# A Mamba recurrence regrouped: 4 states x 32 channels per partition instead of 2 states x 64

## The chip, the cores and the metric

One core of a Trainium2 chip runs the whole layer. The metric is the device time of one launch in microseconds, the median over runs. TensorE is written PE below, VectorE DVE, ScalarE ACT, GpSimd POOL, and SP is the engine that issues most DMAs.

## The reference

A layer for 2,048 tokens of width 512: a layernorm, then `x + mamba(xn) + moe(xn)`, with a mixture of 64 experts (top 6) and a shared expert. The part in question is the mamba recurrence (1,024 channels, 16 states each):

```python
dt = jax.nn.softplus(dt + dt_proj_b)
def step(state, inp):
    dt_t, x_t, B_t, C_t = inp
    dA = jnp.exp(dt_t[..., None] * A)
    dBx = dt_t[..., None] * B_t[:, None, :] * x_t[..., None]
    state = state * dA + dBx
    y = jnp.einsum('bds,bs->bd', state, C_t)
    return (state, y)
...
y = ys.transpose(1, 0, 2) + xt * D
y = y * jax.nn.silu(gate)
```

## The kernel before

Three stages, one behind the other. `stage1` makes the layernorm, the input projection with its convolution and gate, the router and its token lists. `stage2` runs the recurrence and, woven into it, the routed experts. `stage3` makes the shared expert, the output projection and the sum of everything. The change is in `stage2`.

`stage2` has 32 steps: 4 chunks of 512 tokens by 8 tiles of 128 channels. Each step also works off one pair of experts. On PE the loop is `for cc in 2`, in it two copies of a loop over j (4 passes), in it two steps (u = 0, 1) written out; so one pass of the inner loop is two steps, and the code of the two copies lies one behind the other.

A step holds 8 groups (g), each a tile of 128 partitions by 2 x 512. A partition stands for one channel and one residue of the state: 2 parities of the state by 64 channels, and the group says which half of the channels (b) and which pair of states (m). Per group:

- `dBx` (L1025 to 1036) on PE makes the product dt * x * B for the group: 16 fp32 matmuls of 64x64 tiles, 128 columns each, from the transposed dt*x and diagonals of B into one of two buffers `p_dBx`. It waits for the scan of g-2. Each fp32 matmul is two MATMUL records and two LDWEIGHTS records in the profile.
- ACT makes `dA` = exp(A * dt) (L937) from `dt_halves`, and saves the last column of the state (`state_carry`, L934).
- DVE scans (L842), two instructions a group, into one of four `state` buffers.
- POOL multiplies the state by C (L784) into one of four `h_times_C` buffers; behind group 0 it issues the gather of tokens (L753), behind group 2 the scatter of expert outputs (L765, L769).
- `sum_states` (L1040 to 1047) on PE adds the states with a 0/1 matrix of 128x64 into `p_y`: for each pair of states (m) 4 matmuls of 512 columns, 64 output partitions each.

PE's order in a step i is written out by hand: product 0, sum m=2 of the step before, dt_proj (L985), product 1, the experts' gate (L1005), product 2, sum m=3 of the step before, transpose_h (L1012), product 3, half of `up`, product 4, the other half, product 5, sum m=0, dtx_T (L998), product 6, sum m=1 (it needs POOL's groups 0 to 3), product 7, `down` (L1022), tokens_T (L991).

dt for the next step: dt_proj, softplus on ACT in four operations at g = 3, `next_dt` (L804) on DVE behind scan 2, then `skip` (L818, y += D*x), `next_dtx` (L811) and behind scan 3 `gate` (L824, y * silu(gate)). At g = 6 ACT copies dt into `dt_halves`, each half of the partitions for itself (L892), and issues two DMAs (L897) that bring each half to the other 64 partitions. At g = 7 it takes the transposed dt*x (L902) and makes diagonals of B for the next chunk (L964).

SP issues, per step and in this order, each behind a wait: w_dt and ts of step i+2; w_gate of the next pair; two rows of C (L1385); x for the next dt*x; x and silu(gate) for skip and gate, and the store of the finished y; w_up; w_down.

## Time and profile before

| what | us |
|---|---|
| median of 3 runs | 1509.86 |
| the runs | 1514.99, 1500.84, 1509.86 |
| the profiled execution | 1520.02 |
| its span, first to last instruction | 1518.2 |
| stage 1 | 0 to about 290 |
| stage 2 | about 290 to 1178 |
| stage 3 | about 1187 to the end |
| PE, DVE, ACT, POOL busy over the span | 1393.1, 1101.0, 916.0, 923.9 |

A record of the profile is one instruction; busy time counts overlapping records once, and a group's mean is that of single records, so that side by side tiles have a sum of means far over the busy time. "idle before" is the time in which the engine had nothing running ahead of that group, with what ended it. A step is found in the timeline by PE's products (L1035): eight blocks of 32 matmuls.

### The profile page before, as it was taken

The page shows a single profiled execution, that of the slowest core. Times are in us where ns is not written, and L with a number is a line of the kernel's source. Part 1 is how long each engine was busy: PE and PEld are TensorE (multiplying, and loading weights), DVE is VectorE, ACT ScalarE, POOL GpSimd, SP SyncE. Part 2 cuts the span into 40 slices and gives each one's busy share as a digit, 9 for nine tenths or more (in the row PEclk, how much of TensorE's full clock was granted, in tenths as well). Part 3 has the DMA queues.
Part 4 walks back from the last instruction along what each step waited for, and adds up shares of the span by engine and source line. Part 5 has one row for each costly group of instructions (what it writes and reads, how often), then busy time and mean ns, then how long its engine had stood idle before and what let it go on. Part 6 is the DMA issues. An engine that isn't in the chain of part 4 may idle for free. (4 is left out here: it accounts for less than half of the span.)

```text
span 1518.2 us, 37596 instructions
## 1 busy us (share of the span) xinstructions
PE 1393.1 (92%) x13451; PEld 840.1 (55%) x13451; DVE 1101.0 (73%) x1275; ACT 916.0 (60%) x1944; POOL 923.9 (61%) x570
## 2 busy tenths in 40 slices
PE   5898987599999999999999999999998589999998
PEld 4666765355454444444445454454543367777776
DVE  3679797578888787888878888787886254645454
ACT  3745554387777777777677777777774233333333
POOL 2444345378888888898888888888897021212120
PEclk9999998799999999999999999999999699999999
DMA  6142544758778787777778778787676700303030
GB/s 263 66 191 91 205 161 170 220 177 259 252 236 245 236 258 239 242 249 245 232 242 248 252 243 251 244 271 244 223 226 206 277 17 29 138 28 138 29 137 28
DMA packets 117613, 292.49 MB, mean 193 GB/s; under 512 B 12400, under 2 KB 14192, under 8 KB 115760
## 3 DMA queue, kind: packets, MB, share of 16 engines
q1 hardware_dynamic: 104064, 264.13, 49.5%
q0 software_dynamic: 8208, 18.91, 6.0%
q10 hardware_dynamic: 5280, 8.65, 3.1%
q8 instruction: 36, 0.59, 0.2%
q14 instruction: 25, 0.20, 0.0%
HBM read 226.23 MB, written 56.77 MB: 186 GB/s over the span
## 5 line engine op out<-in xcount | busy, mean ns | idle before, releaser
L842 DVE TENSOR_TENSOR_SCAN state<-dA,state_carry,p_dBx 128x512 f32<-128x512 f32 x512 | 623.3, 1265 | 150.3 <-PE p_dBx L1035 106.8
L784 POOL TENSOR_TENSOR h_times_C<-state,C_bcast 128x1024 f32<-128x1024 f32 x256 | 617.0, 2682 | 65.3 <-DVE state L842 64.9
L937 ACT ACTIVATE dA<-dt_halves,A_par 128x512 f32<-128x512 f32 x512 | 338.9, 709 | 0.0
L1035 PEld LDWEIGHTS p_dBx<-B_diagonals,dt_x_T 64*64 64x64 f32 x8192 | 222.6, 133 | 119.9 <-issue 116.2
L1035 PE MATMUL p_dBx<-B_diagonals,dt_x_T 64*64 64x128 f32 x8192 | 283.8, 276 | 1.2 <-issue 1.2
L1046 PE MATMUL p_y<-h_times_C,sum_over_parity 128*64 128x512 f32 x1040 | 252.2, 606 | 7.7 <-POOL h_times_C L784 7.7
L249 POOL TENSOR_TENSOR w_in_parts_lo<-C_bcast,w_in_parts_hi 128x512 fp32r<-128x512 f32 x64 | 88.9, 1391 | 147.1 <-ACT w_in_parts_hi L439 146.8
L1183 POOL TENSOR_TENSOR moe_part_a<-moe_part_a,moe_part_b 128x2048 f32<-128x2048 f32 x4 | 18.5, 4614 | 175.3 <-DMA moe_part_b<-moe_b 175.3
L1046 PEld LDWEIGHTS p_y<-h_times_C,sum_over_parity 128*64 128x64 f32 x1040 | 63.2, 136 | 107.6 <-issue 91.2
L1213 DVE TENSOR_TENSOR out_parts_lo<-B_diagonals,out_parts_hi 128x512 fp32r<-128x512 f32 (+1 forms) x64 | 64.5, 1018 | 68.2 <-ACT out_parts_hi L1272 68.2
L562 PE MATMUL p_in<-xT_parts_hi,w_in_parts_lo 128*128 128x512 f32 x256 | 75.2, 417 | 26.8 <-ACT silu_gate L465 17.5
L1310 PE MATMUL p_out<-out_parts_hi,out_parts_lo 128*128 128x512 f32 (+1 forms) x224 | 89.4, 399 | 10.8 <-DVE out_parts_lo L1213 10.8
L320 DVE SCALAR_TENSOR_TENSOR conv_out<-conv_in,conv_w,conv_out 128x512 f32<-128x512 f32 x96 | 89.9, 946 | 10.0 <-ACT conv_out L453 7.7
L1022 PE MATMUL p_g<-w_down_pair,expert_h_T 128*64 128x512 f32 (+1 forms) x396 | 92.3, 601 | 0.8 <-DMA w_down_pair<-in_w_down 0.8
L1005 PE MATMUL p_u<-w_up_pair,tokens_T 128*64 128x352 f32 x512 | 89.9, 472 | 0.0
L1272 ACT ACTIVATE out_parts_hi<-B_diagonals 128x512 fp32r<-128x512 f32 (+1 forms) x64 | 39.4, 628 | 83.2 <-PE p_out L1310 83.2
L439 ACT ACTIVATE w_in_parts_hi<-C_bcast 128x512 fp32r<-128x512 f32 x64 | 40.2, 630 | 80.7 <-PE p_in L562 54.2
L1310 PE MATMUL p_out<-out_parts_hi 128*128 128x512 f32 (+1 forms) x224 | 88.3, 394 | 0.0
L1310 PE MATMUL p_out<-out_parts_lo,out_parts_hi 128*128 128x512 f32 (+1 forms) x224 | 88.3, 394 | 0.0
L934 ACT ACTIVATE state_carry<-state 128x2 f32 x256 | 49.9, 195 | 58.3 <-DVE state L842 47.5
L1005 PE MATMUL p_g<-w_gate_pair,tokens_T 128*64 128x352 f32 x512 | 82.8, 466 | 0.0
L1259 ACT ACTIVATE expert_y<-p_shared_g 128x512 f32<-128x512 f32 (+1 forms) x24 | 14.3, 597 | 109.9 <-PE p_shared_u L1300 109.9
(168 smaller groups left out, 2111.4 us busy)
## 6 DMA issues: line engine op xcount, KB each, us to landing
w_gate_pair<-in_w_gate SPq DMA_DIRECT2D x32, 1408.0 KB, 7.2
w_up_pair<-in_w_up SPq DMA_DIRECT2D x32, 1408.0 KB, 8.7
w_down_pair<-in_w_down SPq DMA_DIRECT2D x66, 512.0 KB, 4.3
w_down_pair<-in_w_down SPq DMA_DIRECT2D x33, 384.0 KB, 5.8
dt_halves<-dt_halves ACTq DMA_DIRECT2D x66, 128.0 KB
g_d<-y_gated SPq DMA_DIRECT2D x33, 256.0 KB, 4.8
sz_d<-silu_gate SPq DMA_DIRECT2D x32, 256.0 KB, 2.0
xt_d<-conv_out SPq DMA_DIRECT2D x4, 2048.0 KB, 7.4
```

Source lines behind the costliest of these rows:

```text
L249: pool.tensor_tensor(wp[1][:, n % 2, :], win[:, tile, :], wp[0][:, n % 2, :], ALU.subtract).then_inc(s_wlo, 1)
L320: ins = dve.scalar_tensor_tensor(xt[:, d, :], xr[:, d, k:k + CH], cw[:, d, k:k + 1], xt[:, d, :], ALU.mult, ALU.add)
L562: ins = pe.matmul(pIn[n % 2][:, :], wp[p][:, n % 2, k * P:(k + 1) * P], xp[q][:, c % 2, k, :], start=at == 0, stop=at == len(parts) - 1)
L784: pool.tensor_tensor(hc[:, q, :, :], hb[:, q, :, :], Cb[:, ND * cp + GS * m:ND * cp + GS * m + GS, :], ALU.mult).then_inc(s_hc, 1)
L842: ins = dve.tensor_tensor_scan(hb[:, g % NBUF, s, :], dA[:, g % NBUF, s, :], pB[:, g % 2, :].rearrange("p (t s) -> p s t", s=GS)[:, s, :], ...
L937: ins = act.activation(dA[:, q, s, :], dtr[:, u, b, :], ACT.Exp, scale=A[:, bass.ds(d, 1), GS * g + s:GS * g + s + 1].rearrange("p a b -> ...
L1005: ins = pe.matmul(pX[r, 0:I], xgT[:, k, r], w[:, a, k, :], start=k == 0, stop=k == KH - 1)
L1022: ins = pe.matmul(pG[r, :], hT[0:k, m, r], wd[0:k, a, m, :], start=m == 0, stop=m == len(IK) - 1)
L1035: ins = pe.matmul(out[HD * p:HD * p + HD, half, j, :, :], dtxT[k, u, j * P + HD * b:j * P + HD * b + HD], diag[k, ND * cp + 2 * j + p, GS ...
L1046: ins = pe.matmul(pY[HD * b:HD * b + HD, :], sel[:, :], hc[:, (2 * m + b) % NBUF, s, :], start=m == 0 and s == 0, stop=m == NG // 2 - 1 an ...
L1213: dve.tensor_tensor(kp[1][0:n, k % 2, a, :], src, kp[0][0:n, k % 2, a, :], ALU.subtract).then_inc(s_klo, 1)
L1310: ins = pe.matmul(pO[j][:, :], kp[p][0:n, k % 2, 0, j * P:(j + 1) * P], kp[q][0:n, k % 2, 1, :], start=k == 0 and at == 0, stop=k == NK - ...
```

## The change

Each partition now stands for 4 residues of the state (NB = 4) by 32 channels (DB = 32); a group is a quarter of the channels (b = g % 4) and two of four states of a residue (m = g // 4).

- `dBx`: tiles of 64x32 instead of 64x64; 32 fp32 matmuls a group instead of 16, same 128 columns.
- `sum_states`: the matrix is 128x32; 8 matmuls of 512 columns for one m (four column quarters by two states), two sums a step instead of four: m=1 of the step before behind product 2, m=0 behind product 6. `h_times_C` has eight buffers, four of them in the half of `C_bcast` that is free now, since C takes 4 rows a chunk of 4 residues by 32 partitions instead of 8 rows of 2 by 64.
- D*x goes from DVE to PE: ACT makes a diagonal of D and `skip` multiplies it by x in four matmuls ahead of sum m=0; x stays for it in one of two buffers, and its second load goes away.
- `next_dt` writes dt into SBUF (`dts`), ACT copies each quarter to its place (four copies), and SP issues twelve DMAs of 32 partitions (`spread_dt`) behind the rows of C, instead of two of 64 on ACT. dtx_T no longer waits for the copies.
- dt_proj's operands for odd and even steps lie on different partitions.
- One chunk of the transposed xn is loaded at the end of stage 2 instead of two, three instead of two at the start of stage 3.

```diff
@@ -263,6 +266,7 @@
+            pool.tensor_tensor(sel4[:, :], sel[:, 0:DB], sel[:, DB:HD], ALU.add).then_inc(keep["s_sel"], 1)
@@ -632,23 +636,26 @@
-        ident, sel, gidx, sidx = keep["ident"], keep["sel"], keep["gidx"], keep["sidx"]
+        ident, sel, sel4, gidx, sidx = keep["ident"], keep["sel"], keep["sel4"], keep["gidx"], keep["sidx"]
         diag, Cb, A, Dp, dtb = keep["diag"], keep["C"], keep["A"], keep["D"], keep["dt_b"]
         tile_in, BT, load_C, load_xT = keep["tile_in"], keep["BT"], keep["load_C"], keep["load_xT"]
-        wdt, ts, xa = tile_in.wdt, tile_in.ts, tile_in.xa
+        wdt, ts = tile_in.wdt, tile_in.ts
         s_par, s_xa, s_wdt, s_diag, s_C = keep["s_par"], tile_in.s_xa, tile_in.s_wdt, keep["s_diag"], keep["s_C"]
...
         wd = sb("w_down_pair", [P, 2, len(IK), H])
-        xs, sz = sb("xt_for_skip", [P, CH]), sb("silu_gate_tile", [P, CH])
+        sz = sb("silu_gate_tile", [P, CH])
+        xa = [tile_in.xa, sb("xt_odd_tiles", [P, CH])]
+        Dd = sb("D_diagonal", [P, 2, P])
         zl = sb("dt_ln", [P, CH])
-        dtr = sb("dt_halves", [P, 2, 2, CH])
+        dts = sb("dt_rows", [P, CH])
+        dtr = sb("dt_blocks", [P, 2, NB, CH])
         dtx = sb("dt_x", [P, CH])
...
         hb = sb("state", [P, NBUF, GS, CH])
-        hc = sb("h_times_C", [P, NBUF, GS, CH])
+        hc = [sb("h_times_C", [P, NB, GS, CH])[:, :, :, :], Cb[:, ND:, :].rearrange("p (b s) t -> p b s t", s=GS)]
         carry = sb("state_carry", [P, ND + STEPS, NS])
@@ -687,15 +694,23 @@
             sp.sem_inc(s_gst, 32)
-            sp.sem_inc(s_xs, 32)
+            sp.sem_inc(s_sz, 16)
...
+            def spread_dt(n):
+                sp.wait_ge(s_dt, n + 1)
+                for b in range(NB):
+                    for p in range(NB):
+                        if p != b:
+                            sp.dma_start(dtr[DB * p:DB * p + DB, n % 2, b, :], dts[DB * b:DB * b + DB, :]).then_inc(s_dtr, 16)
+            spread_dt(0)
             load_wd(0)
-            sp.wait_ge(s_dtx, 1)
-            tile_in.load_xa(sp, 1)
+            tile_in.load_xa(sp, 1, xa[1])
             for i in range(STEPS):
@@ -711,32 +726,33 @@
                     load_C(sp, c + 1, d)
-                elif d < 2:
+                elif d < 1:
                     load_xT(sp, d)
-                sp.wait_ge(s_dtx, i + 2)
-                if i + 2 < STEPS:
-                    tile_in.load_xa(sp, i + 2)
-                else:
-                    sp.sem_inc(s_xa, 16)
+                sp.wait_ge(s_dA, NG * i + 1)
+                spread_dt(i + 1)
                 sp.wait_ge(s_g, i + 1)
-                sp.dma_start(xs[:, :], io["xt_d"][i]).then_inc(s_xs, 16)
-                sp.dma_start(sz[:, :], io["sz_d"][i]).then_inc(s_xs, 16)
+                sp.dma_start(sz[:, :], io["sz_d"][i]).then_inc(s_sz, 16)
                 sp.dma_start(io["g_d"][i], gb[:, 1 - i % 2, :]).then_inc(s_gst, 16)
...
                     sp.dma_start(wu[:, :, :, :].rearrange("p a k i -> p (a k i)"), io["sw_up"]).then_inc(keep["s_w3"], 16)
+                sp.wait_ge(s_sum, 2 * i + 3)
+                if i + 2 < STEPS:
+                    tile_in.load_xa(sp, i + 2, xa[i % 2])
+                else:
+                    sp.sem_inc(s_xa, 16)
                 sp.wait_ge(s_yps, i + 2)
...
             sp.dma_start(io["g_d"][STEPS], gb[:, 1, :]).then_inc(s_gst, 16)
-            sp.wait_ge(s_dtr, 32 * (STEPS + 1))
+            sp.wait_ge(s_dtr, 16 * NB * (NB - 1) * (STEPS + 1))
...
             pool.memset(yo[:, :, :], 0.0).then_inc(s_yz, 1)
-            for t in (hh[:, :], wsc[:, :], xs[:, :], sz[:, :], hc[:, :, :, :]):
+            for t in (hh[:, :], wsc[:, :], sz[:, :], hc[0], hc[1]):
                 pool.memset(t, 0.0).then_inc(s_c0, 1)
@@ -778,11 +794,11 @@
                             for g in range(NG):
-                                m, q = g // 2, g % NBUF
-                                pool.wait_ge(s_sum, NG // 2 * i + (m + 1))
+                                m, b, q = g // NB, g % NB, g % NBUF
+                                pool.wait_ge(s_sum, 2 * i + (m + 1))
                                 pool.wait_ge(s_scan, NG * i + (g + 5))
-                                pool.tensor_tensor(hc[:, q, :, :], hb[:, q, :, :],
-                                                   Cb[:, ND * cp + GS * m:ND * cp + GS * m + GS, :], ALU.mult).then_inc(s_hc, 1)
+                                pool.tensor_tensor(hc[m][:, b, :, :], hb[:, q, :, :],
+                                                   Cb[:, NM * cp + GS * m:NM * cp + GS * m + GS, :], ALU.mult).then_inc(s_hc, 1)
                                 if g == GATHER_AT:
@@ -801,30 +817,25 @@
                 dve.wait_ge(s_zl, n + 1)
-                dve.tensor_tensor(pM[:, :], pM[:, :], zl[:, :], ALU.add).then_inc(s_dt, 1)
-            def next_dtx(n):
+                dve.tensor_tensor(dts[:, :], pM[:, :], zl[:, :], ALU.add).then_inc(s_dt, 1)
+            def next_dtx(n, u):
...
                 by_row = "p (i j r) -> p i j r"
-                dve.tensor_tensor(dtx[:, :].rearrange("p (j i r) -> p i j r", i=2, j=JD), pM[:, :].rearrange(by_row, i=2, j=JD),
-                                  xa[:, :].rearrange(by_row, i=2, j=JD), ALU.mult).then_inc(s_dtx, 1)
-            def skip(n, d):
-                dve.wait_ge(s_sum, NG // 2 * n + 2)
-                dve.wait_ge(s_xs, 32 * n + 32)
-                dve.scalar_tensor_tensor(pY[:, :], xs[:, :], Dp[:, d], pY[:, :], ALU.mult, ALU.add).then_inc(s_yd, 1)
+                dve.tensor_tensor(dtx[:, :].rearrange("p (j i r) -> p i j r", i=2, j=JD), dts[:, :].rearrange(by_row, i=2, j=JD),
+                                  xa[u][:, :].rearrange(by_row, i=2, j=JD), ALU.mult).then_inc(s_dtx, 1)
...
                 dve.wait_ge(s_gst, 16 * n + 16)
-                dve.wait_ge(s_yd, n + 1)
+                dve.wait_ge(s_sz, 16 * n + 16)
+                dve.wait_ge(s_sum, 2 * n + 2)
                 dve.tensor_tensor(gb[:, u, :], pY[:, :], sz[:, :], ALU.mult).then_inc(s_g, 1)
             next_dt(0)
-            next_dtx(0)
+            next_dtx(0, 0)
             dve.wait_ge(s_c0, CLEARED)
@@ -846,8 +857,7 @@
                                 next_dt(i + 1)
-                                skip(i, bass.ds(2 * j + (u + ND - 1), 1))
-                                next_dtx(i + 1)
+                                next_dtx(i + 1, 1 - u)
                             if g == DT_AT + 1:
@@ -882,19 +891,19 @@
-            def dt_halves(n, u, used):
-                act.wait_ge(s_dtx, n + 1)
+            def dt_blocks(n, u, used):
+                act.wait_ge(s_dt, n + 1)
...
-                for b in range(2):
-                    own = slice(b * HD, b * HD + HD)
-                    ins = act.activation(dtr[own, u, b, :], pM[own, :], ACT.Copy)
+                for b in range(NB):
+                    own = slice(DB * b, DB * b + DB)
+                    ins = act.activation(dtr[own, u, b, :], dts[own, :], ACT.Copy)
...
-                act.wait_ge(s_dtc, n + 1)
-                for b in range(2):
-                    own, other = slice(b * HD, b * HD + HD), slice((1 - b) * HD, (2 - b) * HD)
-                    act.dma_start(dtr[other, u, b, :], dtr[own, u, b, :]).then_inc(s_dtr, 16)
+            def D_diagonal(u, d):
+                act.activation(Dd[:, u, :], ident[:, :], ACT.Copy, scale=d).then_inc(s_Dd, 1)
@@ -916,7 +925,8 @@
-            dt_halves(0, 0, None)
+            D_diagonal(0, Dp[:, 0:1])
+            dt_blocks(0, 0, None)
@@ -926,9 +936,10 @@
                         d = 2 * j + u
-                        act.wait_ge(s_dtr, 32 * i + 32)
+                        act.wait_ge(s_dtc, i + 1)
+                        act.wait_ge(s_dtr, 16 * NB * (NB - 1) * i + 16 * NB * (NB - 1))
                         for g in range(NG):
-                            q, b = g % NBUF, g % 2
+                            q, b = g % NBUF, g % NB
                             row, at = (i + (ND - 1), g + NG - NBUF) if g < NBUF else (i + ND, g - NBUF)
@@ -957,7 +968,7 @@
-                                dt_halves(i + 1, 1 - u, NG * i + 1)
+                                dt_blocks(i + 1, 1 - u, NG * i + 1)
@@ -965,6 +976,8 @@
                                 ins.then_inc(s_diag, 1)
+                                act.wait_ge(s_sum, 2 * i + 1)
+                                D_diagonal(1 - u, Dp[:, bass.ds(d + 1, 1)])
@@ -993,7 +1008,6 @@
-                pe.wait_ge(s_dtc, n + 1)
@@ -1026,25 +1040,31 @@
                 pe.sem_inc(s_past, 1)
-                b, m = g % 2, g // 2
+                m, b = g // NB, g % NB
                 out = pB[:, g % 2, :].rearrange("p (i j r s) -> p i j s r", i=2, j=JD, s=GS)
...
                         k = slice(HD * half, HD * half + HD)
-                        for p in range(2):
-                            ins = pe.matmul(out[HD * p:HD * p + HD, half, j, :, :], dtxT[k, u, j * P + HD * b:j * P + HD * b + HD],
-                                            diag[k, ND * cp + 2 * j + p, GS * m * HD:GS * (m + 1) * HD].rearrange("k (s r) -> k s r", s=GS),
+                        for p in range(NB):
+                            at = (p % 2 * NM + GS * m) * HD
+                            ins = pe.matmul(out[DB * p:DB * p + DB, half, j, :, :], dtxT[k, u, j * P + DB * b:j * P + DB * b + DB],
+                                            diag[k, ND * cp + 2 * j + p // 2, at:at + GS * HD].rearrange("k (s r) -> k s r", s=GS),
                                             start=True, stop=True)
...
+            def skip(i, u):
+                pe.wait_ge(s_g, i + 1)
+                pe.wait_ge(s_Dd, i + 1)
+                for b in range(NB):
+                    own = slice(DB * b, DB * b + DB)
+                    pe.matmul(pY[own, :], Dd[:, u, own], xa[u][:, :], start=True, stop=False, skip_group_check=True)
             def sum_states(i, m, steps_ago):
-                pe.wait_ge(s_hc, NG * i + (2 * m + 6 - NG * steps_ago))
-                if m == 0:
-                    pe.wait_ge(s_g, i + 1)
+                pe.wait_ge(s_hc, NG * i + (NB * m + 8 - NG * steps_ago))
                 for s in range(GS):
-                    for b in range(2):
-                        ins = pe.matmul(pY[HD * b:HD * b + HD, :], sel[:, :], hc[:, (2 * m + b) % NBUF, s, :],
-                                        start=m == 0 and s == 0, stop=m == NG // 2 - 1 and s == GS - 1, skip_group_check=True)
+                    for b in range(NB):
+                        ins = pe.matmul(pY[DB * b:DB * b + DB, :], sel4[:, :], hc[m][:, b, s, :],
+                                        start=False, stop=m == 1 and s == GS - 1, skip_group_check=True)
                 ins.then_inc(s_sum, 1)
@@ -1061,7 +1081,6 @@
                             dBx(i, cp, u, 0)
-                            sum_states(i, 2, 1)
                             dt_proj(i + 1, 1 - u, half + u)
@@ -1069,7 +1088,7 @@
                             dBx(i, cp, u, 2)
-                            sum_states(i, 3, 1)
+                            sum_states(i, 1, 1)
                             transpose_h(i)
@@ -1078,17 +1097,16 @@
                             dBx(i, cp, u, 5)
-                            sum_states(i, 0, 0)
                             dtx_T(i + 1)
                             dBx(i, cp, u, 6)
-                            sum_states(i, 1, 0)
+                            skip(i, u)
+                            sum_states(i, 0, 0)
                             dBx(i, cp, u, 7)
...
                             tokens_T(i + 1, 1 - u, half + u)
-            sum_states(STEPS, 2, 1)
-            sum_states(STEPS, 3, 1)
+            sum_states(STEPS, 1, 1)
             transpose_h(STEPS)
@@ -1148,7 +1166,7 @@
-            for c in range(2, NCH):
+            for c in range(1, NCH):
@@ -1345,8 +1363,9 @@
-        sp.dma_start(self.wdt[:, u, :], self.io["w_dt"][i % ND]).then_inc(self.s_wdt[u], 16)
-        sp.dma_start(self.ts[:, u, :], self.io["ts_d"][i // ND]).then_inc(self.s_wdt[u], 16)
+        r = slice(RANK * u, RANK * u + RANK)
+        sp.dma_start(self.wdt[r, :], self.io["w_dt"][i % ND]).then_inc(self.s_wdt[u], 16)
+        sp.dma_start(self.ts[r, :], self.io["ts_d"][i // ND]).then_inc(self.s_wdt[u], 16)
@@ -1379,10 +1399,10 @@
-            at, own = ND * (c % 2) + a, slice(c * CH, c * CH + CH)
-            for p in range(2):
-                row = NS + ND * p + a
-                sp.dma_start(keep["C"][p * HD:p * HD + HD, at, :], io["bc_d"][row:row + 1, own].to_broadcast([HD, CH])).then_inc(keep["s_C"], 16)
+            m, own = a // 2, slice(c * CH, c * CH + CH)
+            for p in (2 * (a % 2), 2 * (a % 2) + 1):
+                row = NS + NM * p + m
+                sp.dma_start(keep["C"][p * DB:p * DB + DB, NM * (c % 2) + m, :], io["bc_d"][row:row + 1, own].to_broadcast([DB, CH])).then_inc(keep["s_C"], 16)
```

## Rows read from the trace of the kernel before

**Rows 1.** Windows view, one step: us, then PE, PEld, DVE, ACT, POOL busy (records)
```profile
869.62:896.40 26.78, 26.57 (x346) 13.24 (x345) 22.39 (x22) 20.33 (x48) 23.10 (x15) 1.00 0.76 244
```

**Rows 2.** The page's groups: busy, mean ns, idle before them and its releaser
```profile
L842 DVE TENSOR_TENSOR_SCAN state<-dA,state_carry,p_dBx 128x512 f32<-128x512 f32 x512 | 623.3, 1265 | 150.3 <-PE p_dBx L1035 106.8
L784 POOL TENSOR_TENSOR h_times_C<-state,C_bcast 128x1024 f32<-128x1024 f32 x256 | 617.0, 2682 | 65.3 <-DVE state L842 64.9
...
L1046 PE MATMUL p_y<-h_times_C,sum_over_parity 128*64 128x512 f32 x1040 | 252.2, 606 | 7.7 <-POOL h_times_C L784 7.7
```

**Rows 3.** Timeline of one step: start, length, engine, line, operation, idle before and releaser
```profile
896.41 1.10 PE L1035 MATMUL p_dBx<-B_diagonals,dt_x_T 64*64 64x128 f32 x32
...
897.79 2.45 DVE L842 TENSOR_TENSOR_SCAN state<-dA,state_carry,p_dBx 128x512 f32<-128x512 f32 x2 [1.79 <-PE p_dBx L1035]
...
900.32 2.36 POOL L784 TENSOR_TENSOR h_times_C<-state,C_bcast 128x1024 f32<-128x1024 f32 x1 [1.01 <-DVE state L842]
...
904.72 2.38 POOL L784 TENSOR_TENSOR h_times_C<-state,C_bcast 128x1024 f32<-128x1024 f32 x1
...
907.82 2.38 POOL L784 TENSOR_TENSOR h_times_C<-state,C_bcast 128x1024 f32<-128x1024 f32 x1 [0.73 <-DVE state L842]
...
913.96 12.16 POOL L784 TENSOR_TENSOR h_times_C<-state,C_bcast 128x1024 f32<-128x1024 f32 x5
...
916.88 1.94 PE L1046 MATMUL p_y<-h_times_C,sum_over_parity 128*64 128x512 f32 x8 [0.20 <-POOL h_times_C L784]
...
918.75 1.10 PE L1035 MATMUL p_dBx<-B_diagonals,dt_x_T 64*64 64x128 f32 x32
...
919.78 2.80 PE L1022 MATMUL p_g<-w_down_pair,expert_h_T 128*64 128x512 f32 x12
...
923.19 1.10 PE L1035 MATMUL p_dBx<-B_diagonals,dt_x_T 64*64 64x128 f32 x32
```

**Rows 4.** Timeline of 711.37 to 711.42, matmuls started within it
```profile
711.38 0.34 PE L1035 MATMUL p_dBx<-B_diagonals,dt_x_T 64*64 64x128 f32 x4
```

**Rows 5.** DMA queues, code fetches in 520:574, in 730:784, in 784:838
```profile
q8 instruction: 5, 0.08, 0.6%
...
q8 instruction: 7, 0.11, 0.8%
...
q8 instruction: 1, 0.02, 0.1%
```

**Rows 6.** Timeline at the jump back of the outer loop
```profile
733.51 0.75 PE L991 MATMUL p_u<-identity,tokens_of_pair 128*128 128x128 f32 x4
735.46 1.10 PE L1035 MATMUL p_dBx<-B_diagonals,dt_x_T 64*64 64x128 f32 x32 [1.20 <-issue]
```

**Rows 7.** Same step: ACT's copies, DMA issues; and DMA view of 896:924, median us to landing
```profile
910.03 1.18 ACT L892 ACTIVATE dt_halves<-p_dt 64x512 f32<-64x512 f32 x2
...
911.24 1.13 ACTq L897 DMA_DIRECT2D dt_halves<-dt_halves  x2
...
904.45 1.12 SPq L1385 DMA_DIRECT2D C_bcast<-bc_d  x2
...
914.16 0.43 SPq L1343 DMA_DIRECT2D w_up_pair<-in_w_up  x1
...
w_gate_pair<-in_w_gate SPq DMA_DIRECT2D x1, 1408.0 KB, 7.5
...
C_bcast<-bc_d SPq DMA_DIRECT2D x2, 128.0 KB, 7.2
xt_for_dtx<-xt_d SPq DMA_DIRECT2D x1, 256.0 KB, 3.7
```

**Rows 8.** Timeline at the start of stage 2 and of stage 3
```profile
291.41 0.52 POOL L740 MEMSET xt_for_skip<- 128x512 f32 x1
...
292.35 3.51 POOL L740 MEMSET h_times_C<- 128x4096 f32 x1
...
1205.12 1.28 ACT L1259 ACT_TABLE_LOAD   x1 [14.23 <-DMA w_out<-in_w_out]
```

37 lines of the change are left out of this document (21 added, 16 removed).

## The prediction

> **What bounds the kernel now.** The change touches only the middle stage (32 steps), a few memsets and copies ahead of it and the loads behind it, so I read the other stages only for their first waits. The windows view of one step gives the load: a step takes 26.78 us, TensorE is busy for 26.57 of them, DVE 22.39, ACT 20.33, POOL 23.10 [rows 1]. The groups on the page say who waits: the scans (L842) wait on the products of TensorE (L1035), POOL's multiplication (L784) on the scans, and TensorE waits for POOL in front of L1046 for 7.7 us in all [rows 2]. Those 7.7 us are small, but they decide: a full engine that still waits once a step is in a loop with the others. The timeline of one step [rows 3] shows that loop, times from the product of g = 0 at 896.41:
>
> - the first scan starts 1.38 later (897.79) and ends about 2.45 on; POOL's first multiplication starts at 900.32, the second at 904.72 (the gather stands between them), the third at 907.82 (0.73 of waiting for scan 2 ahead of it), the fourth at 913.96 (the scatter stands between);
> - the sum that needs the fourth starts at 916.88, having waited 0.20 us. Behind it come the last product (918.75), `down` (919.78), the next tokens, and the next step's first product at 923.19: 6.31 us.
>
> 20.47 + 6.31 = 26.78. TensorE's total and this loop are equally long, so taking work off TensorE alone gains only until the loop holds it.
>
> **Sums in column quarters.** A sum of 8 records (4 fp32 matmuls of two records) costs 1.87 (916.88 to 918.75 [rows 3]) with two 64-column tiles side by side: about four records one after the other, 0.43 each, and a fill of 0.16. Four 32-column tiles should put 16 records into the same 1.87. A step has two such groups instead of four: minus 3.74. No 32-column tile is in the trace; the bounds are 1.87 a group (full overlap) and 3.74 (none beyond today's). I take 1.87, as two tiles already overlap fully.
>
> **D*x on TensorE.** Eight records in four tiles: 2 x 0.43 = 0.86, at most 1.7. It stands ahead of the last sum, where TensorE will wait for POOL anyway (below); with that cover gone it costs 0.86 x 31 = 27 us. DVE loses the skip, 0.7 us off its 22.4, which is not the bound.
>
> **Products in 64x32 tiles.** Each of the 8 products has 64 record pairs instead of 32. Today 32 pairs take 1.03 (918.75 to 919.78): 8 rounds of four tiles. The timeline of 0.05 us at the start of one shows four matmuls started within it [rows 4], so starting a matmul costs about 0.01 us, and eight tiles a round add some 0.03. Bounds: 1.03 (8 rounds again) and 2.06 (today's 32 ns a record holds for each). I take 1.06, because four tiles start close together and then work side by side; eight need no more rounds. The Trainium skill (TensorE: Matmul & The Clock Gate, "Wait — 56ns, not 53.3ns?") says starts never come closer than about 25 ns, which would make a product at least 1.6; [rows 4] show closer starts for four tiles, and nothing shows it for eight.
>
> **TensorE's load after**: 26.57 - 3.74 + 0.86 + 8 x 0.03 = 23.9 us. POOL's own chain, first to fourth multiplication 13.64 without 0.73 of waiting, and five in 12.16 [rows 3], is 25.1. DVE 21.7. ACT: two more copies (1.18 for two [rows 7]), a diagonal (0.3), minus the 1.13 for two DMA issues: 20.33 + 1.5 busy. None is over the loop.
>
> **The loop after.** Of the sums at products 0, 2, 5 and 6 those at 2 and 6 stay. Without the one behind product 0, product 2 comes 1.87 sooner, scan 2 follows scan 1 at once, and POOL's third multiplication starts when its second ends (904.72 + 2.38 = 907.10) instead of 907.82: 0.72 saved. From there all is as before: scatter, fourth multiplication, sum of 1.87, product, `down`, tokens. Less 2 x 0.03 for the two products in the loop, 0.66 a step; over 31 steps **-20.5 us**. TensorE's other freed time turns into its wait for POOL ahead of the last sum (about 2 us a step, which hides D*x).
>
> **The twelve transfers.** They leave ACT's queue and go to SP's, behind w_gate and C. An issue takes 0.56 (1.12 for two C transfers [rows 7]): 12 are 6.7 us. dt is ready about 10 us into a step, so the last is issued at about 17 and lands 3.7 to 7.2 later (x 3.7, C 7.2 [rows 7]): at 20.5 to 24. ACT wants it at about 22 for a first use that DVE has only at 27.4. Behind it on SP: silu(gate), the g store, w_up (today issued at 914.16, 17.8 into the step [rows 7], now about 18), then x and w_down, which wait for later events anyway. Cost 0; if all landed at 24 and more, ACT's three dA and the tokens' copy would come a microsecond or two late, up to 1 x 31 = 31 us.
>
> **Instruction supply.** Two steps (one pass of the inner loop) are 2 x (346 + 345) = 1,382 TensorE records today [rows 1]. After: 2 x (256 + 8) more matmuls and as many weight loads, 2,438. The trace shows that this matters. The queue q8 that fetches 16 KB pieces of code is at work with seven packets in the two steps behind the jump back to the outer loop's start (731 us), with five where the second copy of the inner loop begins (520 us), with one in the repeat at 784 [rows 5]. So a repeat of 1,382 is served from a buffer, and a jump over two copies (2,764) isn't. Behind that jump TensorE stood idle 1.20 us [rows 6]. 2,438 lies nearer to the length that missed, so I take it that every jump back now misses: 3 in each of 4 runs of the inner loop, 12 in all. Each costs 1.20 by that row; the longer last product keeps the sequencer back by some 0.4 more, the inner jump has 0.4 less register work than the outer. 12 x 1.20 = **+14.4 us**, all of it inside the loop (between `down` and the next first product). Bounds: 0 (it fits) and 12 x 4.6 = 55 (no cover: 1.20 and the 3.41 from `down` to the next first product). The Trainium skill (Runtime: NRT & Kernel Launch, "Instruction fetch mechanics") gives TensorE room for 2,048 instructions; by that 2,438 misses, and the trace brackets it without deciding.
>
> **Start and end.** h_times_C is now two buffers of 4096 elements: one more memset of 3.5, less 0.52 for the buffer dropped [rows 8]; the gather of the first tokens stands behind it on POOL: **+3**. The last stage loads one more chunk of xn_T (1,024 KB) ahead of w_out, on which ACT waited 14.23 us [rows 8]: between 0 and 5.5 (w_gate's 1,408 KB land in 7.5 [rows 7]), **+3** in between.
>
> **Sum.** 1518.2 - 20.5 + 14.4 + 3 + 3 = 1518.1. The median of three runs is 1509.86, 0.7% under the profiled run of 1520.02; the same ratio gives **1510 us**: no difference. About 1% is what a measurement of this kernel can tell from none (the three runs spread over 0.9%).
>
> **Rivals.**
> 1. The longer loop fits the buffer: no 14.4. 1495. For it: only the gap between 1,382 and 2,764. 12%, and it is just 1% faster.
> 2. Slower: the product in eight tiles costs more. It is decided at one place: with x more per product TensorE's total is 23.9 + 8x, the loop 26.12 + 2x; from x = 0.33 the step is over today's, from 0.37 the total leads. At 2.06 (x = 1.0) a step is 31.9: +5.1 x 31, some 1670; at the 1.6 of the skill's rule about 1590. For it: no eight-tile row exists. Against: [rows 4]. 20%.
> 3. The last product, twice as long in records, keeps the sequencer so far back that nothing covers the jump, 4.6 each: +41, 1551; with half of the cover 1530. 10%.
> 4. dt's transfers land late, or another wait comes in ahead of the loop: +0.3 to 1 us a step, 1520 to 1540. 13%.
> 5. The forecast, 1495 to 1522: 45%.
>
> **Range and chances.** 1488 to 1552 holds cases 1, 3, 4, 5; only 2 is left out. Faster by over 1%: half of case 1 and a part of 5 (a jump that costs less), 0.17. Within 1%: most of 5, half of 1, a little of 4: 0.48. Slower: 2, 3 and most of 4: 0.35.
>
> **What the profile after would show.** Products: time from one's start to the next block 1.06, 64 pairs. Sums: 16 records in 1.87. TensorE idle about 2 us ahead of the last sum of a step, released by POOL. POOL's third multiplication directly behind its second. Two-step windows of 52.2 us plus 1.2, with five or more fetch packets in each, and an idle time put down to issue ahead of every second first product. If packets stay at a few, case 1 holds. If TensorE is full and products take over 1.4, case 2. If dA waits for the dt blocks, case 4.

## The result, and the profile after

| | before | after |
|---|---|---|
| median | 1507.71 us (4 runs, 1500.84 to 1514.99) | 1652.51 us (4 runs, 1649.43 to 1668.16) |
| profiled span | 1518.2 us | 1653.5 us |
| ratio, 95% interval | | 1.098 (1.089 to 1.107) |

The changed kernel is 9.8% slower. The prediction was 1510, no difference. A step, 26.78 us before [rows 1], now takes 28 to 36, from one first product (g = 0) to the next.

From the page of after: the granted clock, the queue that fetches code, and the groups that answer to [rows 2]; the last row is the product's group before:

```profile
PEclk9999997799899989898899999999999789999999
...
q8 instruction: 185, 3.03, 0.7%
...
L853 DVE TENSOR_TENSOR_SCAN state<-dA,state_carry,p_dBx 128x512 f32<-128x512 f32 x512 | 624.2, 1262 | 231.1 <-PE p_dBx L1050 189.0
L1050 PE MATMUL p_dBx<-B_diagonals,dt_x_T 64*32 64x128 f32 x16384 | 342.2, 283 | 118.9 <-issue 81.5
...
L1035 PE MATMUL p_dBx<-B_diagonals,dt_x_T 64*64 64x128 f32 x8192 | 283.8, 276 | 1.2 <-issue 1.2
```

DVE stands idle 231 us ahead of its scans instead of 150, 189 of them for products instead of 107. TensorE stands idle 119 us ahead of products instead of 1.2, and 81 of those are put down to issue: the trace shows nothing that was missing. That leaves code as the suspect: 185 packets of 16 KB were fetched (3.03 MB); before it was 36. The timeline of TensorE around one jump back of its inner loop (start, length, engine, line, operation, idle before it and its releaser):

```profile
983.10 1.06 PE L1060 MATMUL p_y<-xt_odd_tiles,D_diagonal 128*32 128x512 f32 x8
...
983.99 1.90 PE L1066 MATMUL p_y<-h_times_C,sum_over_states 128*32 128x512 f32 x16
...
985.82 1.16 PE L1050 MATMUL p_dBx<-B_diagonals,dt_x_T 64*32 64x128 f32 x64
...
986.90 2.80 PE L1036 MATMUL p_g<-w_down_pair,expert_h_T 128*64 128x512 f32 x12
...
989.63 0.75 PE L1006 MATMUL p_u<-identity,tokens_of_pair 128*128 128x128 f32 x4
...
994.03 1.17 PE L1050 MATMUL p_dBx<-B_diagonals,dt_x_T 64*32 64x128 f32 x64 [3.65 <-issue]
...
995.13 2.07 PE L1000 MATMUL p_dt<-ts_tile,w_dt 32*128 32x512 f32 x2
...
998.86 1.96 PE L1050 MATMUL p_dBx<-B_diagonals,dt_x_T 64*32 64x128 f32 x62 [1.10 <-issue]
...
1000.75 3.11 PE L1019 MATMUL p_g<-w_gate_pair,tokens_T 128*64 128x352 f32 x16
```

The tiles do what was forecast: D*x 0.89 (983.10 to 983.99), a sum of 16 records 1.83, a product of 64 pairs 1.08 (985.82 to 986.90). What is new stands in the brackets: 3.65 idle at the jump (1.20 in [rows 6]), then the next product breaks off after two of its 64 records and goes on at 998.86. The window of that stretch, and two windows of 200 us ahead of it, the second of which runs into it (length, busy time of PE, PEld, DVE, ACT and POOL with records, granted clock, DMA share, GB/s):

```profile
995.10:1001.80 6.70, 5.60 (x75) 2.70 (x72) 3.14 (x3) 3.84 (x7) 2.96 (x3) 0.50 0.33 85
...
600.00:800.00 200.00, 173.32 (x3764) 86.80 (x3764) 150.90 (x133) 134.56 (x308) 148.61 (x89) 0.91 0.70 214
800.00:1000.00 200.00, 168.02 (x3774) 84.83 (x3778) 145.98 (x128) 140.09 (x318) 145.94 (x86) 0.94 0.71 211
```

Behind the idle time the granted clock is 0.50, the lower of its two levels (1.2 GHz). In the kernel before it is 1.00 in all three windows.

### The profile page after: what moved, and what is told of

Read it like the earlier page. It is cut to its first block and busy times, and to the rows that moved or that the text cites. A ratio compares the mean times of both kernels' runs of the same rounds, so it can differ in the third digit from the quotient of the medians.

```text
span 1653.5 us, 54715 instructions
## 1 busy us (share of the span) xinstructions
PE 1398.2 (85%) x21899; PEld 848.9 (51%) x21899; DVE 1151.8 (70%) x1242; ACT 970.5 (59%) x2043; POOL 944.8 (57%) x571
## 3 DMA queue, kind: packets, MB, share of 16 engines
q8 instruction: 185, 3.03, 0.7%
## 5 line engine op out<-in xcount | busy, mean ns | idle before, releaser
L1050 PE MATMUL p_dBx<-B_diagonals,dt_x_T 64*32 64x128 f32 x16384 | 342.2, 283 | 118.9 <-issue 81.5
L800 POOL TENSOR_TENSOR h_times_C<-state,C_bcast 128x1024 f32<-128x1024 f32 x128 | 318.6, 2497 | 155.7 <-DVE state L853 155.2
L1050 PEld LDWEIGHTS p_dBx<-B_diagonals,dt_x_T 64*32 64x32 f32 x16384 | 249.5, 109 | 267.9 <-issue 264.8
L948 ACT ACTIVATE dA<-dt_blocks,A_par 128x512 f32<-128x512 f32 x512 | 339.1, 710 | 0.0
L800 POOL TENSOR_TENSOR C_bcast<-state,C_bcast 128x1024 f32<-128x1024 f32 x128 | 314.3, 2642 | 24.4 <-DVE state L853 24.1
L1231 DVE TENSOR_TENSOR out_parts_lo<-B_diagonals,out_parts_hi 128x512 fp32r<-128x512 f32 (+1 forms) x64 | 60.0, 948 | 72.9 <-ACT out_parts_hi L1290 72.9
L1019 PE MATMUL p_g<-w_gate_pair,tokens_T 128*64 128x352 f32 x512 | 101.8, 550 | 0.0
L1019 PE MATMUL p_u<-w_up_pair,tokens_T 128*64 128x352 f32 x512 | 93.6, 474 | 3.6 <-issue 3.5
L901 ACT ACTIVATE dt_blocks<-dt_rows 32x512 f32<-32x512 f32 x132 | 82.3, 624 | 1.7 <-DVE dt_rows L820 0.5
L1066 PE MATMUL p_y<-C_bcast,sum_over_states 128*32 128x512 f32 x528 | 72.7, 606 | 11.2 <-issue 9.4
```

The costliest lines, as they stand in the source:

```text
L800: pool.tensor_tensor(hc[m][:, b, :, :], hb[:, q, :, :], Cb[:, NM * cp + GS * m:NM * cp + GS * m + GS, :], ALU.mult).then_inc(s_hc, 1)
L901: ins = act.activation(dtr[own, u, b, :], dts[own, :], ACT.Copy)
L948: ins = act.activation(dA[:, q, s, :], dtr[:, u, b, :], ACT.Exp, scale=A[:, bass.ds(d, 1), GS * g + s:GS * g + s + 1].rearrange("p a b -> ...
L1019: ins = pe.matmul(pX[r, 0:I], xgT[:, k, r], w[:, a, k, :], start=k == 0, stop=k == KH - 1)
L1050: ins = pe.matmul(out[DB * p:DB * p + DB, half, j, :, :], dtxT[k, u, j * P + DB * b:j * P + DB * b + DB], diag[k, ND * cp + 2 * j + p // 2 ...
```

## The experiments

Ratios are to runs of the kernel before made beside it on the same chip, with 95% intervals. "One run" means that the kernel ran once, without an interval.

### How long may the loop be? half8, half6, half12

```
-                        for p in range(NB):
+                        for p in range(2 if g in (2, 3, 4, 5) else NB):   # half8; half6: (2,3,4); half12: (2..7)
```

> Of the changed kernel, in four of the eight products of a step (g = 2 to 5) half of the column tiles is left out (p = 2 and 3), so part of dt*B*x is not computed. Two steps of TensorE's inner loop are then 1,988 instructions by my count of the listing (a fp32 matmul counts as 4 of 64 bytes) instead of some 2,500. Theory, instruction supply: the loop is now held in TensorE's instruction buffer, the queue q8 falls from 185 packets to under 50, the stalls inside products and behind the jumps go, and the time falls from 1652 to about 1505 (1490 to 1520). Rival, eight-tile products are dear by themselves: a quarter of the product work is gone, so a quarter of the 142 us: about 1617, and packets play no part.

> The same with half of the tiles left out in three products of a step only (g = 2 to 4): 2,116 instructions in two steps, 128 more than in half8. Theory, instruction supply with an edge between the two lengths: the loop is fetched anew in each pass, over 130 packets on q8, and most of the stalls stay: about 1620 (1590 to 1650). If the loss were only a matter of how much is fetched, it would stand close to half8. Rival, dear products: 3/16 of the 142 us gone, 1626, but then half8 must be near 1617 as well; the difference between half6 and half8 decides: over 80 us for the edge, 9 us for the rival.

> The changed kernel with half of the column tiles (p = 2 and 3) left out in six of eight products (g = 2 to 7), so part of dt*B*x is not computed. half8's pass is 962 matmuls and as many weight loads, 1,980 instructions with registers and waits, and is still fetched anew (4 to 7 us at each jump back). This one has 834 of each, some 1,724. If what counts is that the pass is over about 1,900, it now fits: under 50 packets, 1495 to 1530. If loops much over today's 1,440 never fit (a buffer of 1,536 or so), over 120 packets and some 1590.

half8: 1.0726 (1.0704 to 1.0749), 1627.0, 153 packets. half6: 1.098 (1.0924 to 1.1036), 1663.5, 166 packets. half12, one run: 1559.39 beside 1511.3, 67 packets. None of the three came out as expected. I had expected half8 to fit; it doesn't: in the trace's branch records all of its 12 inner jumps still hold the sequencer, the part of TensorE that hands out its instructions, for 3.6 to 7.5 us, as all 12 do in the changed kernel (3.6 to 6.4, 2,491 instructions a pass). half6 lies above its range of 1590 to 1650. In half12, with 1,724 instructions in a pass, nine of twelve jumps take 0.21 to 0.25 again, as all do in the kernel before (1,439 instructions), and three about 5.8. So a pass of 1,439 is always held, one of 1,724 mostly, and one of 1,980 never.

Code comes in pieces of 256 instructions (shown under "Jump or stream?"), and a pass that starts in the middle of a piece touches one more. The trace gives the places: in half12 the first copy of the loop touches eight pieces and loses three of six jumps, the second touches seven and loses none; in half8 they touch nine and eight, and every jump is lost. That speaks for room for seven pieces that are sure to stay, from these two kernels alone. The Trainium skill (Runtime: NRT & Kernel Launch, "Instruction fetch mechanics") gives TensorE 2,048 instructions, which is eight pieces, and says that the next piece is fetched while the present one runs. Read as the length of a loop that stays, the 2,048 is too much by the measurement: 1,980 never stay.

The other reading, that each product costs in proportion to its tiles, wants 9 us between half6 and half8, where the edge wanted over 80; it was 36, which decides for neither. It wants about 1600 for half12 (three eighths of 142 us gone), and that took 1559. It falls with the next kernel.

### The same work in a shorter loop: short

TensorE's inner loop has one step a pass (about 1,270 instructions) instead of two. For this what TensorE reads must lie at one address, so each double buffer becomes a single one, conv_out is loaded twice, and some loads, ACT's copies and waits move with them:

```
-                        for u in range(2):
-                            i = ND * c + (2 * j + u)
+                        with pe.Fori(0, 2) as u:
+                            i = ND * c + (2 * j + u)
-        dtxT = sb("dt_x_T", [P, 2, JD * P])
+        dtxT = sb("dt_x_T", [P, JD * P])          # likewise w_dt, ts_tile, tokens_of_pair, D_diagonal
```

> The changed kernel with one step instead of two in a pass of TensorE's inner loop: 609 matmuls and weight loads of 64 bytes each way, about 1,270 instructions, as many as before or fewer. To that end all that TensorE reads lies in one buffer instead of two (dt's operands, the tokens, dt*x transposed, D's diagonal), and conv_out is loaded twice, for dt*x and for the skip. All products, sums and the D*x matmuls are those of the changed kernel. Theory, instruction supply: the pass stays in the buffer, under 45 packets on q8, the product 1.1 us each time, jumps back about 0.2, and the time is what the working without jumps gives: 1495 to 1520, ratio 0.985 to 1.005. Rival, eight-tile products or the other moved work are dear: 1650 as in the changed kernel, since none of that work is gone. Rival, late dt transfers: a part of the 142 us stays, 1550 to 1600.

1549.13, ratio 1.0234 (1.0196 to 1.0272), 34 packets. Its inner jumps back take 0.21 to 0.25. All products, sums and D*x are there, and 7.5% are gone, so eight-tile products by themselves aren't the loss. But it isn't 0.985 to 1.005. Most of its steps take 27.3, not 26.1.

### Jump or stream? after_straight, before_straight

```
-                    with pe.Fori(0, ND // 2) as j:
+                    for j in range(ND // 2):
```

> The changed kernel with TensorE's inner loop written out (8 steps straight, twice): no taken jump inside, and every instruction is fetched once or twice in all in the stage. Theory: two costs, the jumps (12 of 3.6 to 6.4 us instead of under 0.3) and the steady stream (stalls inside products where a new 16 KB piece is not there in time). Straight code leaves only the second: steps like those without a jump, 28 us, 32 x 3 less than now: about 1570 (1550 to 1610). If only the jumps cost, 1510 to 1520. If the jumps cost nothing, 1652.

> The kernel before with TensorE's inner loop written out in the same way: its 1,382 records for two steps are now fetched all the time (over 150 packets instead of 36), but one piece of 16 KB lasts for about 9.6 us of work instead of 5.5. Theory (the stream fails when pieces are used up faster than they come): no loss, 1500 to 1520. Rival (any fetching stalls, whatever its rate): a loss of the same kind as in the changed kernel, 5.6 stalls in two steps, over 1560.

after_straight: 1593.16, 1.0483 (1.0438 to 1.0528), 169 packets. before_straight: 1520.12, 1.0002 (0.9981 to 1.0023), 104 packets. The product's group in each, first after_straight:

```profile
L1050 PE MATMUL p_dBx<-B_diagonals,dt_x_T 64*32 64x128 f32 x16384 | 345.0, 282 | 101.9 <-issue 67.5
```

and before_straight:

```profile
L1035 PE MATMUL p_dBx<-B_diagonals,dt_x_T 64*64 64x128 f32 x8192 | 283.5, 276 | 9.5 <-DVE state L842 6.4
```

Fetching by itself costs nothing: with all of its code streamed the kernel before is as fast as in a loop. The changed kernel loses 67.5 us to issue ahead of products though it never jumps back inside. So there are two costs: the inner jumps, 1.098 - 1.048 = 5.0%, some 75 us (the twelve hold the sequencer for 60 us in all), and what is left in straight code, 1.048 - 1.023 = 2.5%, some 38 us (after_straight against short, which differ in their buffers too). In two steps TensorE takes 9 packets (804 to 858) where before_straight takes 6. A product of 64 pairs passes 128 records in 1.08 us, one of 32 pairs 64 in 1.03 [rows 3]: code is used twice as fast just where the pauses are. A piece of the stream, after_straight:

```profile
829.40 1.14 PE L1050 MATMUL p_dBx<-B_diagonals,dt_x_T 64*32 64x128 f32 x62
833.54 0.40 PE L1050 MATMUL p_dBx<-B_diagonals,dt_x_T 64*32 64x128 f32 x2 [3.00 <-issue]
```

Here a product stops two records short of its end for 3.00 us. The order of the records shows what it waits for. In after_straight products break 71 times for over 0.4 us in the stage. 38 of these breaks, 57 us in all, lie whole multiples of 256 instructions apart in each of the two straight stretches, and each ends 1.20 to 1.61 us behind the end of a packet of the code queue. 256 instructions are thus one piece of 16 KB, and the product waits for the next one. In the changed kernel 46 of 47 such breaks, 62 us, are of this kind; before_straight has none. The other 33 of after_straight, 19 us, fit neither the pieces nor the queue and nearly all lie within 1 us of an indirect DMA's issue on POOL (see "What makes products pause"): a part of the 38 us is theirs and not the stream's. The Trainium skill (Runtime: NRT & Kernel Launch, "Instruction fetch mechanics") calls the crossing of a 16 KB boundary "mostly hidden"; that holds for before_straight (1.0002) and not for after_straight (3.00 us at one crossing).

### Where short's other microsecond goes: short_dtp, after_dtp

The rows of dt*x, with minimum/median/maximum in ns: before,

```profile
L811 DVE TENSOR_TENSOR dt_x<-p_dt,xt_for_dtx x33: 680/684/692, 296.5 to 1150.0; 128x512 f32<-128x512 f32 x33
```

after,

```profile
L827 DVE TENSOR_TENSOR dt_x<-dt_rows,xt_for_dtx x17: 693/3284/3325, 293.2 to 1278.8; 128x512 f32<-128x512 f32 x17
L827 DVE TENSOR_TENSOR dt_x<-dt_rows,xt_odd_tiles x16: 2316/2322/3342, 318.1 to 1250.5; 128x512 f32<-128x512 f32 x16
```

The change moved dt from p_dt (PSUM) to dt_rows (SBUF), where the transfers can read it, and dt*x, the same 128x512, went from 0.68 to 2.3 and 3.3 us. In short's timeline:

```profile
876.73 4.72 POOL L807 TENSOR_TENSOR h_times_C<-state,C_bcast 128x1024 f32<-128x1024 f32 x2
...
878.66 3.35 DVE L834 TENSOR_TENSOR dt_x<-dt_rows,xt_for_dtx 128x512 f32<-128x512 f32 x1
...
884.52 1.51 PE L1057 MATMUL p_dBx<-B_diagonals,dt_x_T 64*32 64x128 f32 x64 [1.98 <-DVE state L860]
...
887.46 1.15 PE L1057 MATMUL p_dBx<-B_diagonals,dt_x_T 64*32 64x128 f32 x64 [0.84 <-DVE state L860]
...
888.54 1.06 PE L1068 MATMUL p_y<-xt_for_skip,D_diagonal 128*32 128x512 f32 x8
```

dt*x ends at 882.01, 0.56 behind POOL's third multiplication (881.45), and takes 3.35 us beside it. The scans behind it are late, products 5 and 6 wait for the scans, and D*x starts at 888.54, when POOL's fourth multiplication is nearly done (888.58): it now lies ahead of the sum in full. The Trainium skill (SBUF — State Buffer, "Who interferes with whom") says this: a DVE instruction with two SBUF inputs contends with a GpSimd instruction that reads SBUF. The trace agrees: 3.35 us beside POOL, against 0.68 with one input in PSUM. The edit writes dt once more into PSUM and lets dt*x read it there:

```
+                dve.wait_ge(s_dt, n + 1)
+                dve.tensor_tensor(pM[:, :], pM[:, :], zl[:, :], ALU.add).then_inc(s_dt2, 1)
-                ... dts[:, :].rearrange(by_row, i=2, j=JD),
+                ... pM[:, :].rearrange(by_row, i=2, j=JD),
```

> short, with dt kept in PSUM as well: DVE adds it twice, once into dt_rows for the transfers and once into p_dt, and dt*x reads p_dt as in the kernel before, so one of its two inputs comes from PSUM. short itself has no lost jump (34 packets) and yet needs 27.3 us a step, not the 26.1 of the working. Theory: its dt*x, now with both inputs in SBUF, takes 3.33 us instead of 0.68, since it ends 0.5 behind POOL's multiplication instead of running beside it, and the scans, products 5 and 6 and D*x behind it come late by that, so that D*x is not covered any more. With p_dt as input dt*x takes 0.7 (one more add of 0.67 beside it), and the step 26.1 to 26.5: 1549 minus 0.8 to 1.2 x 31, 1512 to 1524. Rivals: D*x or the copies of dt's blocks are the cause: 1549 as in short.

> The changed kernel with the same one edit (dt also in PSUM, dt*x reads it there), its loop as long as it was. Theory of two causes that add: 1652 minus 20 to 38: 1615 to 1635. If TensorE's waits for instructions cover the late dt*x, no change: 1645 to 1655.

short_dtp: 1540.68, 1.0173 (1.0139 to 1.0207). after_dtp: 1641.44, 1.0848 (1.0775 to 1.0921). dt*x is back at 0.69 in all 33 cases, which shows that the second SBUF input was its cause. The gain is only 0.6%, though (1.3% in the long loop; in both pairs the intervals overlap), and both times lie above the ranges that I had expected. In short_dtp 15 of 31 steps take 27.8 us or more and the others 26.4 to 26.7, one 27.6. A piece of short_dtp:

```profile
869.48 5.67 SPq L710 DMA_DIRECT2D dt_blocks<-dt_rows  x9
...
871.52 1.47 POOL L793 DMA_INDIRECT moe_a<-expert_y,scatter_rows  x1 [0.81 <-POOL scatter_rows L789]
871.62 1.00 PE L1060 MATMUL p_dBx<-B_diagonals,dt_x_T 64*32 64x128 f32 x39
...
873.08 0.42 PE L1060 MATMUL p_dBx<-B_diagonals,dt_x_T 64*32 64x128 f32 x4 [0.46 <-issue]
...
873.29 1.42 POOL L793 DMA_INDIRECT moe_b<-expert_y,scatter_rows  x1 [0.30 <-issue]
873.85 0.31 PE L1060 MATMUL p_dBx<-B_diagonals,dt_x_T 64*32 64x128 f32 x2 [0.35 <-issue]
...
874.60 0.80 PE L1060 MATMUL p_dBx<-B_diagonals,dt_x_T 64*32 64x128 f32 x19 [0.43 <-issue]
```

A product in four pieces, 3.7 us instead of 1.08, and no code is fetched. It lies beside the scatter's two issues on POOL and SP's row of transfers. This is product 5, and it is broken like this in 28 of 32 steps, long and short ones (this step takes 26.7); in short it took 1.27 from first to last matmul (median), in short_dtp 3.45. My expectation for short_dram puts these pauses in the long steps alone, and that was misread: what the long ones have beside them is one more pause, in product 6 (1.54 instead of 0.89). 11 of the 15 have it and none of the others; the other four stand at a change of chunk or at the start.

### What makes products pause: no_scatter, few_spreads, short_dram

```
# no_scatter, in scatter(n): for the 32 steps of the loop
+                if not isinstance(n, int):
+                    return
# few_spreads, in spread_dt(n)
-                        if p != b:
+                        if p != b and (n < 2 or p == (b + 1) % NB):
# short_dram
-  12 x sp.dma_start(dtr[DB * p:DB * p + DB, n % 2, b, :], dts[DB * b:DB * b + DB, :])
+  sp.dma_start(io["dt_d"][n], dts[:, :])
+  4 x sp.dma_start(dtr[DB * p:DB * p + DB, n % 2, :, :], io["dt_d"][n].rearrange("(b r) t -> r b t", b=NB))
```

> short_dtp without the scatter of the expert outputs in steps 0 to 31 (only the last two are added to moe_a and moe_b), the waits on it dropped; everything else is computed. If POOL's scatter is needed for the pauses, the product of g = 5 takes 0.89 us first to last in nearly every step, none has three pauses. POOL is then 4 us lighter a step: about 25 us a step, 1480 or below. If SP's twelve issues alone cause them, the pauses stay.

> short_dtp with four instead of twelve dt transfers a step from the third step on, so two of three foreign blocks of dt keep old values; everything else is computed. If SP's issues are needed for the pauses, the product of g = 5 takes 0.89 us in nearly every step and the time is 1505 to 1520. If POOL's scatter alone causes them, three pauses of 0.6 in half of the steps stay and the time is near 1540.

> short_dtp, with the twelve transfers of dt's rows between partitions and ACT's four copies replaced by one store of dt to DRAM and four loads from there: 5 DMA issues on SP a step instead of 12 for the same data. In short_dtp dt*x is 0.69 us again, but about half of the steps are 28.1 us and the rest 26.4 to 26.7: in the long ones the product of g = 5 takes 3.5 us from first to last matmul instead of 0.89, with three or four pauses of 0.57 to 0.85 us in it, 0.7, 1.7 and 2.4 us behind the issue of POOL's scatter and with the 12 issues of SP going on in that time, one every 0.62 us; no code is fetched then. Theory: the pauses come from SP's run of issues while POOL issues its scatter; with the issues gone they go, and all steps are 26.1 to 26.7: 1540 minus 20 to 25, 1510 to 1525. Rival: SP's issues have no part in it (POOL's scatter or the scan beside it alone): the pauses stay, 1535 to 1545. Rival: the loads from DRAM are late: ACT waits for dt_blocks at the start of each step, above 1540.

no_scatter, one run: 1495.27 beside 1516.4; not one pause in the products of g = 5 and 7 (median 0.92 and 0.89 from first to last matmul), steps 25.36. few_spreads, one run: 1509.97; one pause stays in product 5 (1.6 from first to last, 3.45 in short_dtp, 0.89 when undisturbed), steps 26.0. So POOL's scatter is needed, and with fewer transfers of dt on SP there are fewer pauses. I had taken the two for alternatives. Whether SP's issues count or the data that they move isn't told apart by this run, nor is a count of pauses for each issue. short_dram: 1693.6, 1.1184 (1.1144 to 1.1223): fewer issues, but the loads land late and ACT waits for them 7.62 us in a step (its third theory); its product 5 still takes 2.2. Why TensorE's issue should stop for this, and only in products of eight tiles (the kernel before has product 5 beside the same scatter and two issues of SP with no pause), stays open.

A step of few_spreads, as a window, and its last sum:

```profile
872.10:898.10 26.00, 24.78 (x627) 12.72 (x612) 22.62 (x22) 21.80 (x51) 23.10 (x15) 1.00 0.78 247
...
891.12 1.92 PE L1079 MATMUL p_y<-h_times_C,sum_over_states 128*32 128x512 f32 x16 [0.40 <-POOL h_times_C L810]
```

26.00 us at full clock, close to the 26.12 that the prediction worked out, and the sum behind D*x waits for POOL, as its loop has it. The step still has one pause in it and lacks eight transfers, so a part of the closeness is luck.

### The scatter's place, and a version faster than both

```
-GATHER_AT, SCATTER_AT = 0, 2
+GATHER_AT, SCATTER_AT = 0, 3      # ..._sc3;  0, 4 in ..._sc4
```

> short with POOL's scatter one multiplication later (behind the fourth instead of the third), so that it no longer stands ahead of the multiplication that the first sum needs. The loop product, scan, multiplications, sum, last product, down is then shorter by about the scatter (2 to 4 us), and the step is bound by the load of POOL (at most 25.1 us) or TensorE (23.9): 1465 to 1490, ratio 0.965 to 0.98. If the loop is not what sets the step of short, no change against it.

> The kernel before with the same move of the scatter alone. TensorE is busy for 26.57 of 26.78 us of a step there, so the shorter loop can give 0.2 x 31 = 6 us at most: ratio 0.995 to 1.0. If it gave more, the improvement of short_sc3 would not need the change at all.

> short_dtp with POOL's scatter behind the fourth multiplication. In short the same move made it 34 us slower, with dt*x at 3.4 us. Theory: there the gap that dt*x and POOL's multiplications fought over was the scatter's place; with dt*x in PSUM the move helps as first reckoned: the step is bound by POOL's 25.1 or TensorE's load: 25.2 to 25.8, 1485 to 1505, ratio 0.98 to 0.995. Rival: the move is bad in the changed kernel for another reason (the second sum of a step): slower than short_dtp.

> short_dtp with POOL's scatter behind the fifth multiplication, so that it is issued while TensorE is at the last sum, the last product and down, and no longer beside the products of g = 5 and 6, which had the pauses. Theory: a product has pauses only beside the scatter's issue; sums and down do not; the four multiplications of the first half come about 4 us sooner: step 25.3 to 26.3, 1490 to 1510, ratio 0.985 to 0.997. Rival: the last product (g = 7) takes the pauses over: 1525 to 1545.

> The kernel before with POOL's scatter behind the fifth multiplication, the move that took short_dtp from 1.017 to 0.992. Theory: TensorE's load (26.57 us a step) is the bound of the kernel before once its loop is open, so the move gives at most 0.3 us a step as it did behind the fourth (0.9965, 26.50 us): ratio 0.993 to 0.999. If it gave 0.992 or less, the move and not the change would be what made short_dtp_sc4 faster than before.

| kernel | us | ratio (95%) |
|---|---|---|
| before_sc3 | 1506.07 | 0.9965 (0.9938 to 0.9991) |
| before_sc4 | 1516.31 | 0.9998 (0.9977 to 1.0019) |
| short_sc3 | 1583.59 | 1.0479 (1.0432 to 1.0526) |
| short_dtp_sc3 | 1559.25 | 1.0272 (1.024 to 1.0305) |
| short_dtp_sc4 | 1503.40 | 0.992 (0.9898 to 0.9942) |
| short_dtp_sc4 again, beside before_sc4 | 1504.59 | 0.9916 (0.9889 to 0.9942) |

Behind the fourth multiplication the scatter still stands beside products, and the move costs time in short and short_dtp (2.5% and 1.0%), against both of my expectations: in short_dtp_sc3 product 6 takes 2.0 from first to last. short_dram with the same move (short_dram_sc3) was expected at 1480 to 1500 and took 1579.90, 1.0425 (1.0392 to 1.0458): there the move gains 7%, and it stays slower than the kernel before. Why the same move goes both ways is not shown. Behind the fifth the scatter stands beside sum, product 7 and `down`:

```profile
863.26 1.12 PE L1010 MATMUL p_dt<-ts_tile,w_dt 32*128 32x512 f32 x2
864.31 1.16 PE L1060 MATMUL p_dBx<-B_diagonals,dt_x_T 64*32 64x128 f32 x64
865.40 2.59 PE L1029 MATMUL p_g<-w_gate_pair,tokens_T 128*64 128x352 f32 x16
...
881.21 1.90 PE L1077 MATMUL p_y<-h_times_C,sum_over_states 128*32 128x512 f32 x16
...
882.61 1.47 POOL L793 DMA_INDIRECT moe_a<-expert_y,scatter_rows  x1 [0.80 <-POOL scatter_rows L789]
883.04 1.55 PE L1060 MATMUL p_dBx<-B_diagonals,dt_x_T 64*32 64x128 f32 x64
884.38 1.42 POOL L793 DMA_INDIRECT moe_b<-expert_y,scatter_rows  x1 [0.30 <-issue]
```

Steps of 25.8 us, and 0.8% faster than the kernel before, on two chips (the second was forecast at 0.990 to 0.994). Product 7 keeps a pause of 0.4 (1.30 from first to last). The same move gives the kernel before nothing; the best place of the scatter that it was given, before_sc3 at 0.9965, leaves the change an advantage of about 0.5%, with intervals that touch. So the change is worth a little, once three things are mended: the loop's length, dt*x's second SBUF input, the scatter's place.

## Why the prediction was wrong

In ratios, from the forecast up: few_spreads 0.996 (one run), short_dtp 1.017, short 1.023, after_straight 1.048, after 1.098.

- **The bound and the loop of one step** held. before_sc3 opens the loop, the step goes from 26.78 to 26.50 and stops at TensorE's load. With most of the disturbances away the changed step is 26.00 where 26.12 was worked out. The wait for POOL ahead of the last sum, forecast at about 2 us, is not there in the row of after above; in few_spreads it is 0.40 behind D*x.
- **Products, sums, D*x**: 1.06, 1.87 and 0.86 forecast; 1.08, 1.83 and 0.89 measured. Rival 2, the dear product, is refuted by these rows and by short. (Its times were also added up wrong: by its own steps, 31.9 and 28.2 against 26.12, it would have given some 1690 and 1575, not 1670 and 1590.) The 25 ns from start to start that the Trainium skill gives (TensorE: Matmul & The Clock Gate, "Wait — 56ns, not 53.3ns?") don't hold across eight tiles: 1.08 us for 64 pairs is 17 ns each.
- **POOL's third multiplication directly behind its second**: so it is (876.73, 4.72 x2 in short).
- **Instruction supply** is the step that failed. That 2,438 records miss was right. The price was not: 12 jumps at 1.20, +14.4, from the one miss of the trace. They hold the sequencer for 3.6 to 6.4 us each, 60 in all, with 3.65 idle in the row above, and cost some 75 us. I had bounded them by 4.6 each, 55, and gave this 10%. The outer jump's 1.20 is no price for them: its sequencer too was held for 3.56, most of it beside queued work. And I took the code between jumps to be free, because the trace of before shows its first pass through a copy of the loop without loss. At the new density it isn't: up to +38, with 57 us of breaks at the edges of pieces. The idle time then costs again through the clock: the experts' gate takes 3.11 and, at 937.16 of after, 4.18 (granted clock 0.50 and 0.72 in windows that hold their start) instead of the 2.59 of short_dtp_sc4.
- **DVE's work** was given as 0.7 less. The edit of the operand, p_dt to dt_rows, stood in the diff and I priced it at nothing. dt*x takes 1.6 to 2.6 more, and with it falls the cover of D*x: 0.6 and 1.3% by the two pairs of runs.
- **The twelve transfers, cost 0**: they land a little late (ACT waits 0.97 for them in a step of short), and no run shows that this costs anything. What they cost comes another way, with the scatter, as pauses in products: short_dtp to few_spreads, 2.1%, by one run.
- **Start +3, stage 3 +3**: the first product starts at 304.04, before at 304.31, so 0; ACT's wait on w_out is 17.28 instead of 14.23 [rows 8], +3.05.

## What to carry to other kernels

Count the instructions of a loop on TensorE, not only its time: smaller tiles do the same work in more instructions, and a loop that no longer stayed on the chip (here 1,439 instructions always did, 1,724 mostly, 1,980 never) cost up to 7.5%, more than any term of the arithmetic. When a buffer moves from PSUM to SBUF, price again every DVE instruction that reads it beside a busy POOL. And a gain that doesn't show may be there, if a small one: take the disturbances away one at a time before giving it up.
